# Half-height transposes of attention probabilities, moved to the next slot, in a fused decoder layer on TensorE

## The reference, cut to what matters

```python
def attn_layer(x, Wqkv, qs, ksc, Wo):      # 16 heads of 64, windows of 32
    q, k, v = jnp.split(x @ Wqkv, 3, -1)   # then by head
    q = l2norm(q) * qs
    k = l2norm(k) * ksc
    ...                                    # rotary factors on q and k
    out = local_attention(q, k, v)         # each window sees itself and the one before
    return out @ Wo

def local_attention(q, k, v):
    ...
    sim = jnp.einsum('bhwie,bhwje->bhwij', bq, bk2) * QK_SCALE
    sim = jnp.where(mask, -jnp.finfo(sim.dtype).max, sim)
    attn = jax.nn.softmax(sim, -1)
    out = jnp.einsum('bhwij,bhwje->bhwie', attn, bv2)
    return out.reshape(b, h, n, d)

def ffn_layer(x, g, bln, W1, b1, W2, b2):
    ...
    a, gate = jnp.split(xn @ W1 + b1, 2, -1)
    return a * jax.nn.gelu(gate, approximate=False) @ W2 + b2
```

## Time and profile before

| what | us |
|---|---|
| median of 3 runs | 2543.07 (2542.53 to 2543.28) |
| the profiled execution | 2539.95 |
| its span, first to last instruction | 2538.1 |
| TensorE, VectorE, ScalarE, GpSimd busy | 2370.2, 1958.3, 1720.5, 1552.6 |
| mean granted clock of TensorE | 0.985 of 2.4 GHz |

### The profile page before, as it was taken

How to read it: one execution, slowest core, us unless ns; L and a number is a source line. 1 busy time by engine, 2 the same in 40 slices (tenths; PEclk the granted TensorE clock), 3 DMA queues, 4 the chain that set the end, 5 groups by cost and what they waited for, 6 DMA issues and landing times.

```text
span 2538.1 us, 63009 instructions
## 1 busy us (share of the span) xinstructions
PE 2370.2 (93%) x22929; PEld 1578.0 (62%) x22929; DVE 1958.3 (77%) x2967; ACT 1720.5 (68%) x3296; POOL 1552.6 (61%) x1359
## 2 busy tenths in 40 slices
PE   6888789997899999999999999999999999999995
PEld 3555456665466666666666666666666666666664
DVE  4899857776777777777778787777777787787774
ACT  5888545443577777777776776777777777767763
POOL 4777723232666667667666666666676676666662
PEclk8999989999999999999999999999999999999997
DMA  2312110000122122222221221221222222212211
GB/s 73 110 60 64 54 45 1 1 1 9 39 69 62 50 66 69 51 63 61 62 62 51 73 62 50 73 63 50 63 70 53 62 59 65 62 51 73 62 50 48
DMA packets 102906, 140.33 MB, mean 55 GB/s; under 512 B 63040, under 2 KB 63936, under 8 KB 102336
## 3 DMA queue, kind: packets, MB, share of 16 engines
q1 hardware_dynamic: 102848, 139.57, 20.6%
HBM read 56.39 MB, written 1.31 MB: 23 GB/s over the span
## 4 chain that ended last, share of the span: by engine, by line
PE 52%; DVE 16%; issue 5%; ACT 1%; DVEq 1%; DMA 0%; POOL 0%; SPq 0%; POOLq 0%; ACTq 0%
PE f_psA L1751 14%; PE f_psO L1735 9%; PE f_psA L1745 7%; PE f_psD L1755 5%; DVE f_mx L1535 5%; PE f_psS L1715 4%; DVE f_Pr L1542 4%; DVE f_den L1546 3%; PE f_psO L1818 3%; PE f_psS L1697 3%; PE f_psD L1845 3%; PE f_psP L1715 2%; DVE f_x L1592 1%; PE f_psS L1687 1%; DVE f_hT L1558 1%
## 5 line engine op out<-in xcount | busy, mean ns | idle before, releaser
L1751 PE MATMUL f_psA<-f_W,f_xT 128*128 (+1 forms) x1152 | 603.2, 617 | 8.6 <-DVE f_m L1569 5.5
L1344 POOL TENSOR_TENSOR f_Pr<-f_Pr,f_rden 128x384 f32<-128x384 f32 x384 | 310.6, 829 | 484.9 <-DVE f_rden L1548 484.9
L1569 DVE TENSOR_TENSOR f_m<-f_psA,f_tab 128x1024 f32<-128x1024 f32 x384 | 458.8, 1222 | 161.5 <-ACT f_sq L1439 159.0
L1369 POOL TENSOR_TENSOR f_qkr<-f_qkr,f_rn 128x1024 f32<-128x1024 f32 x192 | 360.7, 1897 | 0.1
L1439 ACT ACTIVATE f_sq<-f_psA 128x512 f32<-128x512 f32 x384 | 228.9, 596 | 166.1 <-PE f_psA L1751 161.2
L1361 POOL TENSOR_TENSOR f_qkr<-f_m 128x512 f32<-128x512 f32 x192 | 245.3, 1278 | 142.8 <-DVE f_m L1569 142.8
L1751 PEld LDWEIGHTS f_psA<-f_W,f_xT 128*128 128x128 f32 x1152 | 184.3, 190 | 147.5 <-DVE f_m L1569 70.5
L1735 PE MATMUL f_psO<-f_PT,f_V 96*64 96x64 f32 x6144 | 261.5, 228 | 4.3 <-ACT f_PT L1414 0.2
L1735 PEld LDWEIGHTS f_psO<-f_PT,f_V 96*64 96x64 f32 x6144 | 211.1, 138 | 69.1 <-issue 54.7
L1535 DVE TENSOR_REDUCE f_mx<-f_psS 128x8 f32<-128x768 f32 x192 | 178.8, 931 | 89.0 <-PE f_psS L1697 89.0
L1362 POOL TENSOR_TENSOR f_qkr<-f_m 128x512 f32<-128x512 f32 x192 | 243.3, 1267 | 0.0
(11 more groups left out here) (166 smaller groups left out, 4578.4 us busy)
## 6 DMA issues: line engine op xcount, KB each, us to landing
f_V<-f_Vt SPq DMA_DIRECT2D x96, 384.0 KB, 4.2
f_V<-f_Vt SPq DMA_DIRECT2D x96, 256.0 KB, 3.6
f_W<-in_f_W SPq DMA_DIRECT2D x48, 344.0 KB, 3.6
m_Cb<-m_BC_rows SPq DMA_DIRECT2D x64, 256.0 KB, 3.1
f_W<-in_f_W SPq DMA_DIRECT2D x48, 296.5 KB, 4.2
f_V<-f_Vt SPq DMA_DIRECT2D x48, 128.0 KB, 5.4
f_xsA<-xall SPq DMA_DIRECT2D x97, 32.0 KB
f_xsA<-xall SPq DMA_DIRECT2D x97, 31.8 KB
```

The source lines that it names most:

```text
L1344: pool.tensor_tensor(pv, pv, rv.unsqueeze(3).broadcast_to([P, 2, 2, KEYS]), ALU.mult).then_inc(Pr_ready[g][j], 1)
L1369: pool.tensor_tensor(qv, qv, rn[:, j * H:(j + 1) * H].unsqueeze(2).broadcast_to([P, H, DH]), ALU.mult).then_inc(qkr_ready[j], 1)
L1569: dve.tensor_tensor(m12[:, j, :, half].rearrange("p m (h d) -> p m h d", d=DH), psA[n % 2][:, :].rearrange("p (h d) -> p h d", d=DH).unsqu ...
L1751: pe.matmul(psA[n % 2][:, :], xT[:, t, :], weights(i, W_QKV + n * 512, 512), start=True, stop=True).then_inc(A_full[n_fill], 1)
```

## The change

PT becomes [96, 2, 8, 64]: the second index is now the half of the query rows, the third the head. A transpose takes 64 query rows of one head, 64x96 to 96x64; the sixteen of a group go row half by row half in turn, the lower rows to one PSUM bank and the upper to another (`psP` if g == half, else a bank of psS). One call does both halves; it waits for both normalised parts and for S_free[1]. `times_v(g, half, ...)` multiplies all eight heads of one half. Transposes and V product of group 0 move from the end of the slot that computes their scores to the front of the next, where unit wu is the same tile; the calls are spread between projections. The orders of TensorE, ScalarE, VectorE and GpSimd are new; SyncE's is as it was.

```diff
-        PT = sb("f_PT", [KEYS, 2, 4, P])
+        PT = sb("f_PT", [KEYS, 2, 8, HQ])
-        psP = ps("f_psP", [P, 4, P])
+        psP = ps("f_psP", [P, 512])
...
+        def probs_bank(g, half):
+            return psP[:, :] if g == half else psS[:, g, :]
...
+                def transpose_probs(g, unit):
+                    for j in range(2):
+                        pe.wait_ge(Pr_ready[g][j], unit + 1)
+                    pe.wait_ge(S_free[1], unit + 1)
+                    if g == 1:
                         pe.wait_ge(P_free[0][0], unit + 1)
+                    else:
+                        at_least(pe, P_free[1][1], unit)
+                    alone(pe, passed)
+                    for h in range(8):
+                        for half in range(2):
+                            r = slice(half * HQ, half * HQ + HQ)
+                            ins = pe.transpose(probs_bank(g, half)[0:KEYS, h * HQ:(h + 1) * HQ], Pr[r, g, (h % 2) * 4 + h // 2, :], ident[r, r])
+                            if h == 7:
+                                ins.then_inc(P_full[g][half], 1)
+                def times_v(g, half, unit, tile):
+                    pe.wait_ge(P_free[g][half], unit + 1)
...
+                    for h in range(8):
+                        hh_ = 8 * g + h
+                        ins = pe.matmul(psO[(h % 2) * DH:(h % 2) * DH + DH, h // 2, half * HQ:(half + 1) * HQ],
+                                        V96[:, tile, half, hh_ * DH:(hh_ + 1) * DH], PT[:, half, h, :], start=True, stop=True)
```

More of the change, by code:

```diff
@@ L1578, in slot @@
                     table_products(3)
+                if "E" in stages:
+                    dve.wait_ge(ge_ready, (i - 1) * 3)
+                    gated(2)
+                if "A" in stages:
                     dve.wait_ge(squared[3], u + 1)
@@ L1592, in slot @@
                     dve.tensor_tensor(x1[:, t, :], psO[:, 0, :], tile_of(i - 1, t), ALU.add).then_inc(x1_ready, 1)
+                if "E" in stages:
+                    dve.wait_ge(ge_ready, (i - 1) * 3)
+                    gated(0)
+                    gated(1)
                 if "B" in stages:
                     denominators(v, 0)
-                    maximum(v, 1)
-                    less_maximum(v, 1)
                 if "A" in stages:
@@ L1602, in slot @@
                     dve.tensor_scalar(rn[:, H:2 * H], rn0[:, H:2 * H], 1e12, None, ALU.min).then_inc(rn_ready, 1)
[L1603 to L1606, removed]
+                if "B" in stages:
+                    maximum(v, 1)
+                    less_maximum(v, 1)
                 if "C" in stages:
@@ L1612, in slot @@
                     dve.bn_aggr(out=momC[:, :], in_=statC[:, :]).then_inc(momC_ready, 1)
+                if "E" in stages:
+                    dve.wait_ge(w2_full, i - 1)
+                    dve.wait_ge(x1b_ready, (i - 1) * 2)
+                    alone(dve, passed)
+                    dve.tensor_tensor(tiles_of(i - 2), psD[0][:, T2:2 * T2].rearrange("p (t d) -> p t d", d=D), tiles_of(i - 2), ALU.add).then_inc(x2_done, 2)
                 if "B" in stages:
@@ L1619, in slot @@
                     dve.tensor_scalar(hatC[:, t, :], xsC[:, t, :], momC[:, 0:1], rstdC[:, :], ALU.subtract, ALU.mult).then_inc(hatC_ready, 1)
[L1620 to L1624, removed]
             slots(dve, slot)
@@ L1699, in scores @@
                     ins.then_inc(S_full[g], 1)
[L1701 to L1708, removed]
-                        pe.wait_ge(P_free[0][0], unit + 1)
[L1710 to L1714, removed]
-                        ins = pe.transpose(dst[0:KEYS, n, :], Pr[:, g, (h % 2) * 4 + h // 2, :], ident[:, :])
-                    ins.then_inc(P_full[g][j], 1)
@@ L1762, in slot @@
                     project(0)
+                if "E" in stages:
+                    pe.wait_ge(ge_ready, (i - 2) * 3 + 2)
+                    w1(0, 0, a_full)
+                    w1(0, 1, a_full)
+                if "C" in stages:
+                    transpose_probs(0, wu)
+                if "E" in stages:
+                    pe.wait_ge(ge_ready, (i - 1) * 3)
+                    w1(0, 2, a_full)
+                if "A" in stages:
+                    project(1)
+                if "C" in stages:
+                    times_v(0, 0, wu, t)
                 if "D" in stages:
@@ L1820, in slot @@
                 if "B" in stages:
-                    scores(1)
+                    transpose_qk(3)
                 if "A" in stages:
-                    project(4)
                     if "D" in stages:
@@ L1829, in slot @@
                     transpose_tokens(u + 1, i + t, 1 - t)
+                    project(4)
+                if "B" in stages:
+                    scores(1)
+                if "A" in stages:
                     project(5)
-                if "B" in stages:
-                    transpose_probs(0, 0)
-                    transpose_probs(0, 1)
-                    times_v(0, 0)
-                    times_v(0, 1)
                 if "E" in stages:
```

115 lines of the change are left out of this document (47 added, 68 removed).

## The result

| | before | after |
|---|---|---|
| median of the runs, us | 2542.8 (2541.84 to 2543.28) | 2566.35 (2565.43 to 2567.95) |
| ratio, 95% interval | | 1.0094 [1.0076, 1.0111] |
| span of the profiled execution | 2538.1 | 2565.0 |
| one pass of the loop, maximum(0) to maximum(0) | 38.66 | 39.11 |
| of it from slot 1's to slot 0's | 20.12 | 20.14 |

The change made the kernel 0.94% slower; forecast was 0.35% faster.

The account below looks back on a forecast made before the run. TensorE, 93% busy, was not taken as sole owner: a loop across TensorE, VectorE and ScalarE sets the period. Pass 38.67 to 38.47, 46 x 0.2 = 9 us saved: 2534 us, range 2497 to 2567.

Parts of the forecast that it names:

- GpSimd's 26.0 us of work has room: GpSimd's tail would end with norm(1,1) some 12.7 us after the maximum, before the second transposes want it.
- my walk: Step-by-step timing of a pass from maximum(0): 20.02 us slot 1 on, 18.47 slot 0 on, sum 38.49, taken as 38.47.
- Halves on TensorE: Half transposes run side by side at 0.058 us a pair, 1.9 us a pass for 3.5, saving 1.6.
- A (serial): Rival: half transposes run one after another, +0.15 us a pass, 2550; chance 0.11, full-price form (2690) 0.02.
- E: Rival: the 96-column weight load sets the halves' pace, up to 0.080 us a pair, pass 38.62, 2541; chance 0.05.
- Tiling changes: TensorE's array tiling changes go from 22 to 34 a pass, 12 x 0.15 = +1.8 us.
- Waits that go: TensorE's transpose waits behind GpSimd (0.9 and 0.8 us a pass) and gate projections' W1 load wait (1.1) disappear.
- Late k copy: ScalarE copies k only after the first exp, so the second difference ends 0.9 us later in slot 0.
- Table load on the path: Slot 1 on, ScalarE's 1.28 us table load ends at 13.69; VectorE's second product pair waits for square(2), 14.3.
- Edges: The four slots before and after the loop lose and gain a V0 each: nothing, within 2 us.
- B: Rival, slower: scores(1) and maximum(1) wait for ScalarE's late k copy, +23 us, 2566; chance with its like 0.19.
- Rival C: Clearly faster: hand-overs between engines shrink by 0.8 of about 1.9 us a pass, 37.7, -37 us, 2506; chance 0.13.

Follow-up runs that it names:

- e5: Control: the kernel before, only GpSimd's two scale multiplications cut into four pieces each; 2542.98 us, ratio 0.9998.
- e9: The changed kernel, scales whole, hatC on VectorE computed by two instructions of the form that also writes an accumulator; 2489.1 us, ratio 0.9793.
- e8: e1 with the last k copy ahead of the first exp on ScalarE again, its transposes right behind scores(0); 2507.16 us, ratio 0.9861.
- e10: e1 with slot 0's table load behind square(3) instead of ahead of square(2); 2505.97 us, ratio 0.9853.
- e3: The changed kernel's orders, but whole transposes and the V product by heads as before; 2563.78 us, ratio 1.0080.
- e1: The changed kernel, only GpSimd's two scale multiplications cut into four pieces each; 2492.7 us, ratio 0.9803.
- e2: The changed kernel with hatC computed on GpSimd behind its two scales instead of on VectorE; 2562.03 us, ratio 1.0081.
- e4: The kernel before with its orders, only the transposes in halves of 64 rows; 2620.68 us, ratio 1.0310.

## Why the prediction was wrong, step by step

**The step that failed.** "GpSimd's 26.0 us of work has room" treats GpSimd's order as free so long as its results arrive in time. They did arrive. What wasn't costed is what a GpSimd instruction does to VectorE's while both run. The scales were moved into hatC's time, and hatC doesn't appear in my walk at all: it takes 0.31 us in before and TensorE wanted it late. From the second difference to project(2) the walk goes over exp, square(0), the copies and V0, and leaves out VectorE's denominators, hatC and first table product, a path put at nothing. In after, on from slot 0's maximum, V0's last matmul starts at 10.33, the first product ends at 11.46, and project(2) starts at 11.51. The trace of before held the sign in a row that I used: rn at 678 ns for 128x16. In after, with GpSimd idle at that time, the same instruction takes 0.14:

```profile
1518.30 0.14 DVE L1607 TENSOR_SCALAR f_rn<-f_rn 128x16 f32<-128x16 f32 x1
```

In before it starts 79 ns into GpSimd's table instruction (0.73 us) and ends 31 ns after it: held as well (by that one, and not by normalise_probs, as the expectation of e5 has it). An instruction that takes five times what its size explains was to be asked who else was running.

**The loop walk** held most of its places, but two errors of opposite sign lie in it. In us after maximum(0), slot 1 on / slot 0 on:

| | forecast | after | e9 |
|---|---|---|---|
| second difference ends | 7.2 / 6.88 | 6.62 / 6.68 | 6.62 / 6.68 |
| square(0) ends | 9.37 / 8.97 | 8.77 / 8.46 | 8.77 / 8.46 |
| both copies end | 10.57 / 10.17 | 9.74 / 9.42 | 9.74 / 9.42 |
| first products start | not in the walk | 10.54 / 10.25 | 9.89 / 9.34 |
| project(2) starts | | 11.89 / 11.51 | 11.25 / 10.61 |
| square(2) ends | 14.3 / 12.65 | 14.48 / 13.27 | 13.74 / 12.37 |
| last products end | 16.82 / 15.21 | 16.93 / 15.73 | 16.19 / 14.83 |
| next maximum(0) | 20.02 / 18.47 | 20.14 / 18.97 | 19.40 / 18.06 |

First error: instructions of ScalarE that follow each other were charged with their whole record, 0.60 us. The records overlap. Before shows it, in a stretch that I had not printed, and after the same (squares and copies):

```profile
1498.61 0.60 ACT L1439 ACTIVATE f_sq<-f_psA 128x512 f32<-128x512 f32 x1 [0.53 <-PE f_psA L1751]
1499.10 0.58 ACT L1414 ACTIVATE f_PT<-f_psS 96x512 f32<-96x512 f32 x1
1499.58 0.59 ACT L1414 ACTIVATE f_PT<-f_psP 96x512 f32<-96x512 f32 x1
```
```profile
1522.12 0.60 ACT L1439 ACTIVATE f_sq<-f_psA 128x512 f32<-128x512 f32 x1 [0.26 <-issue]
1522.62 0.58 ACT L1414 ACTIVATE f_PT<-f_psP 96x512 f32<-96x512 f32 x1
1523.09 0.59 ACT L1414 ACTIVATE f_PT<-f_psS 96x512 f32<-96x512 f32 x1
1523.57 0.60 ACT L1439 ACTIVATE f_sq<-f_psA 128x512 f32<-128x512 f32 x1
```

Start to start is 0.47 to 0.50, so each of these steps was about 0.12 too long; a pair of products takes 2.34, not 2 x 1.22; and rn was charged at 0.68. In slot 0 on, the copies thus end 0.75 early. From there to square(2)'s end the walk was 0.47 too *short* (2.48 against 2.95 in e9): V0's first half had not run by then, both halves start at 9.41 behind project(1), and project(2) follows the end of the first product (10.55) at 10.61. The net is what the new orders are worth without the hold: 37.46 (e9), 1.0 us less than the 38.47 forecast. Second error: the hold, +1.65. 38.47 - 1.01 + 1.65 = 39.11. In slot 1 the two all but cancel (20.02 forecast, 20.14 found), so that the walk is right there by luck; slot 0 on has less of the first (-0.41) and more of the second (+0.91).

**Halves on TensorE**: right. One group of transposes in after, duration min/median/max of its loads and matmuls (the upper bank's rows are the same):

```profile
L1719 PEld LDWEIGHTS f_psS<-ident,f_Pr x8: 122/123/125, 1508.7 to 1509.1; 64*96 64x96 f32 x8
L1719 PE MATMUL f_psS<-ident,f_Pr x8: 216/216/258, 1508.7 to 1509.1; 64*96 64x64 f32 x8
```

From 1508.68 to the eighth pair at 1509.12 there are seven steps, 0.063 each with the longer first, 0.057 each from the second pair (1508.78) on; 0.058 was forecast. Rivals A (serial) and E fall. "TensorE: Matmul & The Clock Gate" of the Trainium skill, section on LDWEIGHTS, would have had the load of 96 columns, at columns/1.2, set 80 ns; the pairs come at 57, so here the measurement decides. The forecast's 0.058 and 0.080 came from dividing by 8 where the rows have seven steps, and were right by luck: the first step of a run is the longer (0.107 for V, 0.058 each behind it).

**Tiling changes**: 34 a pass for 22, as forecast. "TensorEngine Tiling (Array Packing)" of the Trainium skill, Key Properties, has each drain the array, and the trace agrees with a gap at every one: from one start to the next a change costs 0.09 to 0.10 us more than the stream in front of it, where nothing else is waited for, and the first step behind it another 0.04 to 0.05 (pairs) or 0.10 (a projection, 0.534 for 0.429). That is inside the forecast's 0.10 to 0.20. That TensorE's own sum doesn't shrink held too: the streams, added up over a pass at their paces, fell from about 32.0 to 30.3 us (-1.6, as forecast), and what is left of the pass, gaps and waits, rose from 6.7 to 8.8, of which twelve more changes are 1.8 by the forecast's 0.15.

**Waits that go**: W1's DMA and both GpSimd waits went as forecast. It didn't help, because TensorE doesn't set the period.

**Late k copy**: the second difference ends 0.7 later than in before's 5.96 (0.9 forecast), as a price inside the walk; as a rival it fell by e8. **Table load on the path**: right in place; that its end fits (13.69 forecast, 13.86 found) is the two errors again, since without the hold it ends at 13.13 (e9). e10 shows that no better place is next to it.

**Edges**: "nothing, within 2 us" was +6.6. The last maximum(0) stands 48.4 us before the end in before, 53.45 in after, 51.7 in e3 and 54.5 in e1. It isn't the work that slid out of its slot: W_O behind the last V product starts 13.9 us after that maximum in before and 14.15 in after. It is TensorE's clock. Behind that point it is granted at 0.82 on average in before and at 0.50, 1.2 GHz, in after (columns as in the earlier trace rows, before first), and the same sixteen matmuls of W_O take 3.75 us for 2.02:

```profile
2503.50:2524.40 20.90, 10.39 (x54) 7.75 (x54) 6.10 (x12) 4.93 (x8) 0.41 (x1) 0.82 0.08 20
2503.63 2.02 PE L1818 MATMUL f_psO<-f_W,f_oT 128*128 128x128 f32 x16 [0.79 <-ACT f_oT L1427]
```
```profile
2525.50:2551.00 25.50, 16.00 (x54) 12.45 (x54) 5.96 (x12) 4.84 (x9) 0.41 (x1) 0.50 0.06 17
2525.66 3.75 PE L1822 MATMUL f_psO<-f_W,f_oT 128*128 128x128 f32 x16 [0.78 <-ACT f_oT L1427]
```

W_O, hatC's transposes with the gate projections, and the last W2 are together 4.8 us longer, of the tail's 5.1. In the 14 us ahead of it TensorE had records for 8.8 us in after and for 10.9 in before; that this made the clock fall is not shown.

**The range** held the time (2566 in 2497 to 2567) by luck: its edge came from a rival whose mechanism (B) was another. Rival C, "clearly faster", priced at 37.7 a pass, is near what the orders are worth without the hold, but by records that overlap, not by the hand-overs it names; no run tested these. Its time was also worked out wrong: 37.7 is 0.97 below 38.67, so 45 us and 2498, not 37 us and 2506. The condition that would have turned the sign, another queue against VectorE rather than behind it, was in none of the rivals.

## What to carry to other kernels

When GpSimd's order changes, lay its new instructions over VectorE's timeline: each tensor_scalar on SBUF that starts while a GpSimd instruction runs may last until that one ends, or the next (e1), so the length of GpSimd's instructions is the price, not its load. Look in the trace of before for small VectorE instructions whose time doesn't fit their size, and treat them with short pieces on GpSimd, or with a form that isn't held. And walk a loop with distances from start to start, not with records' lengths.

## What the runs showed of the hardware that I had not expected

- A tensor_scalar of 128x128 on VectorE, 0.31 us alone, takes 1.63 beside a running GpSimd multiply of 1.90, 1.83 when it meets one near its start, 0.91 beside two pieces and 0.77 beside four; it ends 78 to 87 ns after the GpSimd instruction, and in e1 behind the one after that which it met. Even 128x16 is held (0.68 for 0.14).
- The form with an accumulator is recorded as TENSOR_SCALAR_CACHE_REDUCE, 0.33 us, plus a read of 0.08, and runs beside the same multiply undisturbed (0.30 to 0.35 in every slot of e9).
- GpSimd's multiply of 128x1024 costs 1.88 us whole and 2.31 in four pieces (4.62 for eight).
- Instructions of ScalarE in sequence overlap by about 0.12 us, two table products on VectorE by 0.1.
- fp32 transposes of 64 rows in the two row halves of the array, each to its own bank, run side by side: two in 0.057 us, where a full one takes 0.109.
- With TensorE's clock at 1.2 GHz (0.50 in the rows) sixteen fp32 matmuls of W_O take 3.75 us for 2.02 at 2.4 GHz, and a pass in which the granted clock averages 0.96 is 1.4 us longer (e2, e4).
